# A ring of three score units in the attention stage, shared with the transposes

## The chip, the cores and the metric

The kernel runs on one core of a Trainium2 chip, as one launch. A core has a matrix engine (TensorE, PE in the views; its weight loads are the row PEld), a vector engine (VectorE, DVE), a scalar engine for activations (ScalarE, ACT), a general engine (GpSimd, POOL) and a queue that issues DMAs (SyncE, SP). Matrix products land in PSUM, which has eight banks; a bank holds 512 fp32 numbers on each of 128 partitions. The metric is the device time of one execution in microseconds; lower is better. Time before: 2411.94 us, the median of three runs (2408.89 to 2412.17).

## The reference

Four pre-norm residual blocks over x of 2 x 2048 tokens with 256 channels: a linear attention, a mixture of experts, a second attention, a second mixture of experts. The change lies in the second attention, a softmax attention with 16 heads of 16 channels:

```
v = _log_map(mu, x)
q = proj_h(v @ Wq.T); k = proj_h(v @ Wk.T); vv = heads(v @ Wv.T)
sc = (-q0 * k0 + q[..., 1:] . k[..., 1:]) / dh ** 0.5
at = softmax(sc, axis=-1)                  # 2048 x 2048 for each of 2 x 16 heads
out = einsum('bhqk,bhkc->bhqc', at, vv)
return _project(_exp_map(mu, out @ Wo.T))
```

So 32 matrices of 2048 x 2048 scores are made, exponentiated, and multiplied by the values.

## The kernel before, in words

The program is a row of stages with a barrier of all engines between them. `attention` (line 1534) is one stage; the stages before it and after it are not touched.

**Work and tiles.** The stage treats two heads at a time: 16 pairs, p = 0 to 15 (8 head pairs of each of 2 batches). A pair has 32 steps, and a step has two units n = 0 and 1. A unit is 128 keys against 512 queries of both heads, so 128 x 1024 scores in two PSUM banks. In all there are 16 x 32 x 2 = 1024 units. A unit goes through these operations:

- `scores` (L1699): two matmuls of 64 rows each (one for each head) write a unit of psS (L1706).
- ScalarE (L1800): one activation, the exponential, reads the unit from psS and writes it to pexp in SBUF, which has six places.
- `weigh` (L1710), once a step for both its units and two steps later: four products of the exponentials with the values (eight matmul records, since the data is fp32), accumulated in psO over the 16 tiles of keys (L1720). A column of ones among the values makes the denominators.

Step s of a pair has the key tile kt = s // 2 and the query half y = s % 2: both halves of the queries are accumulated side by side, each in its own bank of psO, psO[:, y, :].

**The shift of the softmax.** For each query tile of a later pair, one step makes one matmul of the queries with sums of keys (`means`, L1725, into the single bank psM), and VectorE takes its maximum (`reduce`, L1812). This runs six steps more than one pair ahead (AHEAD, `mean_at`). The sums of four keys each are made by `sum_keys` (L1807), one reduction over 2048 columns at step 10. When the 32 maxima of a pair are there, `make_shift` (L1826) computes the shift with four small operations at step 25 of VectorE's order, at step 28 `turn_shift` (L1748) transposes it on TensorE into psX, `put_shift` (L1838) copies it out, and SP writes it into the queries by two DMAs (L1682), before the pair begins.

**The output.** In step 1 of the next pair `take_out` (L1845) copies both banks of psO to SBUF, one after the other. In steps 3 and 5 `turn_out` (L1756) transposes a half with four transposes into psX, and `divide` (L1852) divides by the denominators and writes the result.

**Side work.** For the pairs 8 to 15, GpSimd (`high`, L1634) and VectorE (`low`, L1864) also split the weights of the last stage in two fp16 parts, one `low` in each of the steps 7, 9, 14, 16, 21 and 23 (SPLIT), with DMAs in and out by SP.

**Order.** The order is written out by hand, for each engine a loop over pairs and steps; every engine carries out its instructions in that order. TensorE's step (L1773 to L1786) is

```
scores(p, step, 0)
weigh(p, step - 2)          # or of the pair before, in steps 0 and 1
scores(p, step, 1)
means(q, n)                 # once a step
turn_out / turn_shift       # in a few steps
```

**Waits around the change.** psS has two units, and unit n of a step always lies in psS[:, n, :]. Before `scores` writes a unit, TensorE waits for the activation of the unit two before it (L1703, the count of `raised`, which starts at 2). `weigh` waits for both activations of its step (L1713) and, at the first key tile, for `take_out` of the bank that it will overwrite. `means` waits for the `reduce` before it (L1730). psX has one bank; the transposes of outputs and of the shift take turns in it, each waiting for `x_free` of the one before. PSUM is full: 4 banks psS, 2 psO, 1 psM, 1 psX.

Ahead of the loop, `first_means` and `first_reduce` make the shift of pair 0 and the first maxima of pair 1, with the banks of psS and psO as three buffers (`early`, L1607).

Of the kernel before, what the change touches and what calls it, by code (L numbers as in the profile page):

```python
# [23 lines left out]
P = 128  # L24
# [1509 lines left out]
def attention(nc, k):  # L1534
# [17 lines left out]
    AHEAD = 6  # L1552
    TURN = ST - 4
    SPLIT, SR = (7, 9, 14, 16, 21, 23), 3
    NSP = len(SPLIT)
# [3 lines left out]
    with Stage(nc, "at") as s:  # L1559
# [8 lines left out]
        inv = s.sb("inv", [P, 4, 4])  # L1568
        psS = s.ps("psS", [P, 2, UN])
        psO = s.ps("psO", [P, 2, BANK])  # L1570
        psM = s.ps("psM", [P, BANK])
        psX = s.ps("psX", [P, BANK])
        (scored, raised, weighed, v_ready, o_out, maxed, reduced, k_ready, shift_in, shifted, x_turned, x_free, chain,
# [22 lines left out]
        def uses():  # L1596
            order = [("shift", 0, 0)]
            for p in range(NPAIR):
                if p:
                    order += [("out", p - 1, 0), ("out", p - 1, 1)]  # L1600
                if p + 1 < NPAIR:
                    order += [("shift", p + 1, 0)]
            return {u: n for n, u in enumerate(order + [("out", NPAIR - 1, 0), ("out", NPAIR - 1, 1)])}

        x_use = uses()

        def early(at):  # L1607

            return (psS[:, 0, :], psS[:, 1, :], psO[:, :, :].rearrange("p a c -> p (a c)"))[at % 3].rearrange(
                "p (h c) -> p h c", h=2)  # L1610

# [9 lines left out]
        with nc.Block() as block:  # L1621
# [31 lines left out]
            def _(sp):  # L1653
# [24 lines left out]
                for p in range(NPAIR):  # L1678
                    sp.wait_ge(x_free, x_use["shift", p, 0] + 1)
                    for hh in range(2):  # L1680
                        row = hh * HR + ROW
                        sp.dma_start(keys(k.QT, p)[row:row + 1, :].rearrange("a (t c) -> a t c", c=P),  # L1682
                                     shiftT[hh * KT16:(hh + 1) * KT16, :]).then_inc(shift_in, 16)
                    if p == HPAIR:

                        sp.wait_ge(raised, 2 + (p - 1) * ST * 2)
# [10 lines left out]
            @block.tensor  # L1697
            def _(pe):
                def scores(p, step, n):  # L1699
                    kt, c = step // 2, (step % 2) * 2 + n  # L1700
                    u = (p * ST + step) * 2 + n

                    pe.wait_ge(raised, u + 1)  # L1703
                    for hh in range(2):
                        r = slice(hh * HR, (hh + 1) * HR)
                        mm = pe.matmul(psS[:, n, hh * BANK:(hh + 1) * BANK], keys(k.KT, p)[r, kt * P:(kt + 1) * P],  # L1706
                                       keys(k.QT, p)[r, c * BANK:(c + 1) * BANK], start=True, stop=True)
                    mm.then_inc(scored, 1)

                def weigh(p, step):  # L1710
                    kt, y = step // 2, step % 2

                    pe.wait_ge(raised, (p * ST + step) * 2 + 4)  # L1713
                    if kt == 0:
                        if p:
                            pe.wait_ge(o_out, 2 * (p - 1) + y + 1)
                        pe.wait_ge(v_ready, p + 1)
                    for g in range(4):
                        n, hh = g // 2, g % 2
                        mm = pe.matmul(psO[g * VW:(g + 1) * VW, y, :], vst[:, p % 2, hh, kt, :],  # L1720
                                       pexp[:, (p * ST + step) % 3 * 2 + n, hh * BANK:(hh + 1) * BANK],
                                       start=(kt == 0), stop=(kt == KT16 - 1))
                    mm.then_inc(weighed, 2)

                def means(p, n):  # L1725
                    if n == 0:
                        pe.wait_ge(k_ready, p + 1)
                    if p * ST + n:

                        pe.wait_ge(reduced, p * ST + n)  # L1730
                    hh, t = n % 2, n // 2
                    r = slice(hh * HR, (hh + 1) * HR)
                    pe.matmul(psM[:, :], keys(k.QT, p)[r, t * P:(t + 1) * P], ksumT[r, p % 2, :],  # L1733
                              start=True, stop=True).then_inc(maxed, 1)

                def first_means(p, t):
                    at = p * KT16 + t
                    if t == 0:
                        pe.wait_ge(k_ready, p + 1)
                    if at >= 3:  # L1740
# [7 lines left out]
                def turn_shift(p):  # L1748
                    pe.wait_ge(shifted, p + 1)
                    use = x_use["shift", p, 0]  # L1750
                    if use:
                        pe.wait_ge(x_free, use)
                    pe.transpose(psX[:, :].bitcast(F16)[0:ST, 0:P], shift[:, :, :].rearrange("p h t -> p (h t)"),
                                 k.identh[:, :]).then_inc(x_turned, 1)

                def turn_out(p, y):  # L1756
                    pe.wait_ge(o_out, 2 * p + y + 1)
                    pe.wait_ge(x_free, x_use["out", p, y])
                    for c in range(4):
                        mm = pe.transpose(psX[:, c * P:(c + 1) * P], oT[:, y, c * P:(c + 1) * P], k.ident[:, :])  # L1760
                    mm.then_inc(x_turned, 1)
# [9 lines left out]
                for p in range(NPAIR):  # L1771
                    pe.wait_ge(shift_in, 32 * (p + 1))
                    for step in range(ST):  # L1773
# [7 lines left out]
                        if q < NPAIR:  # L1781
                            means(q, n)
                        if step in (3, 5) and p:
                            turn_out(p - 1, step // 4)
# [4 lines left out]
                for y in range(2):  # L1789
                    turn_out(NPAIR - 1, y)  # L1790

            @block.scalar
            def _(act):
                act.sem_inc(raised, 2)

                for u in range(NPAIR * ST * 2):
                    act.wait_ge(scored, u + 1)

                    act.wait_ge(weighed, u + 1)
                    act.activation(pexp[:, u % 6, :], psS[:, u % 2, :], ACT.Exp,  # L1800
                                   scale=D ** -0.5 / (QS * QS)).then_inc(raised, 1)

            @block.vector
            def _(dve):
                dve.sem_inc(weighed, 6)

                def sum_keys(p):  # L1807
                    with nc.allow_low_precision(reason="the shift need not be exact"):
                        dve.tensor_reduce(ksumT[:, p % 2, :], keys(k.KT, p).rearrange("p (g m) -> p g m", m=GM),
                                          AX.X, ALU.add).then_inc(k_ready, 1)  # L1810

# [26 lines left out]
                def put_shift(p):  # L1838
                    dve.wait_ge(x_turned, x_use["shift", p, 0] + 1)
                    if p:  # L1840

                        dve.wait_ge(shift_in, 32 * p)
                    dve.tensor_copy(shiftT[:, :], psX[:, :].bitcast(F16)[0:ST, 0:P]).then_inc(x_free, 1)

                def take_out(p, y):  # L1845

                    dve.wait_ge(weighed, 6 + (p * ST + ST - 2 + y + 1) * 2)
                    if p:
                        dve.wait_ge(x_turned, x_use["out", p - 1, y] + 1)
                    dve.tensor_copy(oT[:, y, :], psO[:, y, :]).then_inc(o_out, 1)  # L1850

                def divide(p, y):  # L1852
                    dve.wait_ge(x_turned, x_use["out", p, y] + 1)
                    o = psX[:, :].rearrange("p (c g d) -> p c g d", c=4, g=4)
                    dve.reciprocal(inv[:, :, :], o[:, :, :, D]).then_inc(divided, 1)
# [12 lines left out]

                sum_keys(0)
                for t in range(KT16):  # L1870
                    if t == 2:
                        sum_keys(1)
                    first_reduce(0, t)
# [4 lines left out]
                for p in range(NPAIR):  # L1878
                    for step in range(ST):
                        if step == 1 and p:  # L1880
                            take_out(p - 1, 0)
                            take_out(p - 1, 1)
                        q, n = mean_at(p, step)
                        if q < NPAIR:
                            reduce(q, n)
                            if n == ST - 1:
                                make_shift(q)
                        if step == 10 and p + 2 < NPAIR:
                            sum_keys(p + 2)
                        if step in (3, 5) and p:  # L1890
# [5 lines left out]
                for y in range(2):  # L1896
                    take_out(NPAIR - 1, y)
                for y in range(2):
                    divide(NPAIR - 1, y)

# [452 lines left out]
```

## Time and profile before

| what | value |
|---|---|
| median of three runs | 2411.94 us |
| the profiled execution, its own time | 2414.36 us |
| its span, first to last instruction | 2412.6 us |
| mean granted TensorE clock | 0.938 |
| PE busy in the span | 2079.7 us (86%) |
| ACT busy in the span | 1534.8 us (64%) |
| DVE busy in the span | 1389.4 us (58%) |

The shares are means over stages with different limits, so they don't say what bounds the attention stage; for that one looks at the stretch of this stage by itself. All times are of one profiled execution, counted from the start of its span. A TensorE instruction appears twice: as PEld for its weight load, and as PE for the product. The ends of the products are modelled, so the starts are the better measure of how fast TensorE goes. An activation's record also covers its own latency, and it overlaps the next one's.

### The profile page before, as it was taken

The numbers are of one execution on the slowest core, as the hardware profiler recorded it, in microseconds if no ns is written. First come the engines' busy times: TensorE is split into PE (matmuls) and PEld (weight loads), VectorE is DVE, ScalarE is ACT, GpSimd is POOL, SyncE is SP. The second block draws the span as 40 slices with busy tenths as digits, with TensorE's granted clock in tenths as the row PEclk, the third lists the DMA queues.
The fourth block names the chain that finished last, engine by engine and source line by source line (L and its number), as shares of the span: only waits on it lengthen the run. The fifth ranks groups of instructions, "written<-read, shape, count | busy, mean of one in ns | idle before, by whom it ended". The sixth has DMA issues, their size and how long they took to land. (4 is left out here: it accounts for less than half of the span.)

```text
span 2412.6 us, 43912 instructions
## 1 busy us (share of the span) xinstructions
PE 2079.7 (86%) x13329; PEld 971.6 (40%) x13330; DVE 1389.4 (58%) x2986; ACT 1534.8 (64%) x2495; POOL 440.3 (18%) x678
## 2 busy tenths in 40 slices
PE   5997799950996999999999999999853699999992
PEld 4785455530661222222222222222242476766761
DVE  5567444347786444444445555553156687777774
ACT  2215333223774999999999999999862344444441
POOL 0030366642000000000000000000000134343430
PEclk9998899975996999999999999999976799999996
DMA  5001344443100000000002222222255265555656
GB/s 194 1 1 70 105 148 146 142 144 140 38 24 1 1 1 1 1 1 1 1 19 71 71 71 71 71 71 71 83 180 164 98 178 175 173 176 170 175 168 231
DMA packets 139075, 220.11 MB, mean 91 GB/s; under 512 B 14080, under 2 KB 108464, under 8 KB 138944
## 3 DMA queue, kind: packets, MB, share of 16 engines
q1 hardware_dynamic: 124160, 176.96, 23.6%
q0 software_dynamic: 13632, 37.24, 4.7%
q10 hardware_dynamic: 1152, 4.19, 0.4%
q8 instruction: 78, 1.28, 0.2%
q14 instruction: 53, 0.43, 0.1%
HBM read 161.82 MB, written 52.20 MB: 89 GB/s over the span
## 5 line engine op out<-in xcount | busy, mean ns | idle before, releaser
L1800 ACT ACTIVATE at_pexp<-at_psS 128x1024 f32<-128x1024 f32 x1024 | 964.2, 1023 | 42.9 <-PE at_psS L1706 39.8
L1814 DVE TENSOR_REDUCE at_mx<-at_psM 128x1 f32<-128x512 f32 x474 | 327.5, 691 | 464.3 <-PE at_psM L1733 464.3
L1720 PE MATMUL at_psO<-at_pexp,at_vst 128*32 128x512 f32 x4096 | 546.4, 605 | 0.1
L1706 PE MATMUL at_psS<-l1c_QT,l1c_KT 64*128 64x512 f16 x2048 | 403.6, 387 | 14.4 <-issue 5.6
L1706 PEld LDWEIGHTS at_psS<-l1c_QT,l1c_KT 64*128 64x128 f16 x2048 | 99.4, 92 | 632.4 <-ACT at_pexp L1800 598.9
L2136 PE MATMUL ex_psH<-wide_wgu,ex_xT 128*128 x1278 | 259.9, 357 | 0.2 <-issue 0.2
L2207 DVE SCALAR_TENSOR_TENSOR ex_bias<-ex_psH,top_w_scale,ex_bias 128x456 f32<-128x456 f32 x213 | 147.4, 692 | 76.7 <-PE ex_psH L2136 63.8
L988 POOL DMA_INDIRECT expert_rows<-ex_y,ex_odx x142 | 140.3, 988 | 259.5 <-issue 181.3
L2180 ACT ACTIVATE ex_sg<-ex_bias 128x228 f32<-128x228 f32 x213 | 83.7, 393 | 152.1 <-DVE ex_bias L2207 152.1
L1733 PE MATMUL at_psM<-at_ksumT,l1c_QT 64*128 64x512 bf16 x474 | 179.1, 378 | 0.6
L2136 PEld LDWEIGHTS ex_psH<-wide_wgu,ex_xT 128*128 128x128 f16 x1278 | 124.5, 97 | 111.8 <-issue 3.6
L982 POOL DMA_INDIRECT ex_xg<-normed,ex_idx x142 | 144.7, 1019 | 112.1 <-POOL ex_odx L973 99.3
L2159 PE MATMUL ex_psY<-wide_w2h,ex_hT 114*128 x1278 | 151.3, 272 | 1.1 <-DVE ex_y L2234 0.7
L1061 PE MATMUL ex_psH<-l_w,ex_xT 128*128 x284 | 141.3, 621 | 4.0 <-issue 2.7
L1626 POOL COPY at_vst<-wide_x 128x512 f32<-128x512 f32 x16 | 9.7, 609 | 675.9 <-PE at_psO L1720 675.9
L1720 PEld LDWEIGHTS at_psO<-at_pexp,at_vst 128*32 128x32 f32 x4096 | 80.6, 108 | 125.3 <-issue 123.6
L2159 PEld LDWEIGHTS ex_psY<-wide_w2h,ex_hT 114*128 114x128 f16 x1278 | 124.6, 98 | 15.7 <-issue 1.6
L1130 DVE TENSOR_SCALAR ex_y<-ex_psY,top_wgt 128x256 f32<-128x256 f32 x71 | 34.3, 484 | 139.5 <-PE ex_psY L1079 102.8
L1099 ACT ACTIVATE ex_hT<-ex_psG 128x256 f32<-128x256 f32 x71 | 27.3, 384 | 128.3 <-PE ex_psG L1070 128.3
L2192 ACT ACTIVATE ex_y<-ex_y,top_wgt 128x256 f32<-128x256 f32 x71 | 36.1, 508 | 93.5 <-DVE ex_y L2234 93.5
L2218 DVE TENSOR_TENSOR ex_h<-ex_bias,ex_sg 128x228 f32<-128x228 f32 x213 | 83.1, 390 | 11.1 <-ACT ex_sg L2180 11.0
L1639 POOL TENSOR_SCALAR l1c_KT<-l1c_KT,top_w_scale 128x684 f16<-128x684 f32 (+1 forms) x48 | 40.9, 859 | 245.4 <-DMA l1c_KT<-in_L_ffn_W 232.5
(362 smaller groups left out, 2782.6 us busy)
## 6 DMA issues: line engine op xcount, KB each, us to landing
ex_bias<-in_L_ffn_bg SPq DMA_DIRECT2D x71, 342.0 KB
ex_bias<-in_L_ffn_b SPq DMA_DIRECT2D x71, 342.0 KB
ex_piece<-in_L_ffn_W SPq DMA_DIRECT2D x48, 228.0 KB, 2.6
l1c_KT<-in_L_ffn_W SPq DMA_DIRECT2D x32, 342.0 KB, 3.4
halves<-l1c_KT SPq DMA_DIRECT2D x32, 342.0 KB, 3.3
wide_wgu<-halves SPq DMA_DIRECT2D x8, 1368.0 KB
ex_b<-in_L_ffn_b SPq DMA_DIRECT2D x71, 128.0 KB
normed<-rt_area SPq DMA_DIRECT2D x16, 512.0 KB, 2.6
```

The source lines that it names most:

```text
L982: pool.indirect_dma_start(xg[:, g, :], None, k.xn_d, bass.IndirectOffsetOnAxis(idx[:, g, :], 0)).then_inc(got[g], 16)
L988: pool.indirect_dma_start(k.y_d, bass.IndirectOffsetOnAxis(odx[:, j, :], 0), y[:, j, :], None).then_inc(put[j], 16)
L1061: mm = pe.matmul(psH[:, j, :], xT[:, j, kk, :], k.w13[:, ds(e, 1), kk, :].rearrange("p a c -> p (a c)"), start=(kk == 0), stop=(kk == KC - 1))
L1706: mm = pe.matmul(psS[:, n, hh * BANK:(hh + 1) * BANK], keys(k.KT, p)[r, kt * P:(kt + 1) * P], keys(k.QT, p)[r, c * BANK:(c + 1) * BANK], s ...
L1720: mm = pe.matmul(psO[g * VW:(g + 1) * VW, y, :], vst[:, p % 2, hh, kt, :], pexp[:, (p * ST + step) % 3 * 2 + n, hh * BANK:(hh + 1) * BANK] ...
L1733: pe.matmul(psM[:, :], keys(k.QT, p)[r, t * P:(t + 1) * P], ksumT[r, p % 2, :], start=True, stop=True).then_inc(maxed, 1)
L1800: act.activation(pexp[:, u % 6, :], psS[:, u % 2, :], ACT.Exp, scale=D ** -0.5 / (QS * QS)).then_inc(raised, 1)
L1814: dve.tensor_reduce(mx[:, n:n + 1], psM[:, :], AX.X, ALU.max).then_inc(reduced, 1)
L2136: mm = pe.matmul(psH[:, n, 0:G2].rearrange("p (n c) -> p n c", n=2), xT[:, j, x, kk, :], k.wgu[:, ds(e, 1), kk, :, w, n * HW:(n + 1) * HW] ...
L2159: mm = pe.matmul(psY[:, 0:C], hT[:, j, x, g, :], k.w2h[:, ds(e, 1), w, g, :].rearrange("p a c -> p (a c)"), start=(at == 0), stop=(at == l ...
L2180: act.activation(sg[:, n, :], bias[:, st.slot(1, BR), n, 0, :], ACT.Silu).then_inc(gated, 1)
L2207: dve.scalar_tensor_tensor(hb, psH[:, n, 0:G2].rearrange("p (n c) -> p n c", n=2), k.w_scale[:, 1:2], hb, ALU.mult, ALU.add).then_inc(adde ...
```

## The change

- psS has three units instead of two (RING = 3), used as a ring. The transposes of outputs and of shifts have no bank of their own any more: each takes the next unit of that ring. `uses` lists all uses of the ring in TensorE's order, and `unit_free` waits before each use for whatever used the same unit three uses earlier: the activation if it was scores, `x_free` if it was a transpose.
- A pair's steps go over all 16 key tiles for query half 0 and then for half 1: kt = step % 16, y = step // 16. So psO is one bank, accumulated for one half at a time.
- Half 0 is copied out in step 17 of its own pair, and transposed and divided in step 19; half 1 is copied in step 1 of the next pair, and transposed and divided in step 3. The first `weigh` of a half waits for the copy of the half before it. At the end of the last pair only one half is left.
- `sum_keys` makes a quarter of its columns in each of the steps 5, 6, 8 and 10 (SUMS) instead of all at step 10.
- psM and `means` stay as they are, one matmul a step. PSUM is full again: 6 banks psS, 1 psO, 1 psM. The first activation's waits are counted from zero instead of two.

```
-    psS = s.ps("psS", [P, 2, UN]);  psO = s.ps("psO", [P, 2, BANK]);  psX = s.ps("psX", [P, BANK])
+    psS = s.ps("psS", [P, RING, UN]);  psO = s.ps("psO", [P, BANK])

+    def uses():
+        order = []
+        for p in range(NPAIR):
+            for step in range(ST):
+                order += [("score", p, step * 2), ("score", p, step * 2 + 1)]
+                if step == OUT[1] and p:                # OUT = (19, 3)
+                    order.append(("out", p - 1, 1))
+                if step == OUT[0]:
+                    order.append(("out", p, 0))
+                if step == TURN and p + 1 < NPAIR:      # TURN = 28
+                    order.append(("shift", p + 1, 0))
+        return order + [("out", NPAIR - 1, 1)]

+    def unit_free(use):
+        v = place[use]
+        if v >= RING:
+            kind, p, n = order[v - RING]
+            if kind == "score":
+                pe.wait_ge(raised, p * ST * 2 + n + 1)
+            else:
+                pe.wait_ge(x_free, x_use[kind, p, n] + 1)

     def scores(p, step, n):
-        kt, c = step // 2, (step % 2) * 2 + n
-        pe.wait_ge(raised, u + 1)
+        kt, c = step % KT16, step // KT16 * 2 + n
+        unit_free(use)

     def weigh(p, step):
-        kt, y = step // 2, step % 2
+        kt, y = step % KT16, step // KT16
         if kt == 0:
-            if p:
-                pe.wait_ge(o_out, 2 * (p - 1) + y + 1)
+            if 2 * p + y:
+                pe.wait_ge(o_out, 2 * p + y)

     # VectorE's loop
     if step == 1 and p:
-        take_out(p - 1, 0)
         take_out(p - 1, 1)
+    if step == KT16 + 1:
+        take_out(p, 0)
...
-    if step == 10 and p + 2 < NPAIR:
-        sum_keys(p + 2)
+    if step in SUMS and p + 2 < NPAIR:
+        sum_keys(p + 2, SUMS.index(step), SUMS.index(step) + 1)
-    if step in (3, 5) and p:
-        divide(p - 1, step // 4)
+    if step == OUT[1] and p:
+        divide(p - 1, 1)
+    if step == OUT[0]:
+        divide(p, 0)
```

## Rows read from the trace of the kernel before

**Rows 1.** Busy time by stretch: length, PE, PEld, DVE, ACT, POOL, clock, DMA, GB/s.
```profile
760.76:1738.10 977.34, 967.81 (x6743) 202.35 (x6740) 450.69 (x732) 964.20 (x1024) 49.25 (x62) 1.00 0.12 36
1745.00:2412.00 667.00, 529.09 (x3642) 376.32 (x3640) 480.95 (x1039) 282.68 (x740) 178.80 (x285) 0.90 0.56 173
```
**Rows 2.** Groups of instructions, 755 to 1745: busy, mean ns, idle before.
```profile
L1800 ACT ACTIVATE at_pexp<-at_psS 128x1024 f32<-128x1024 f32 x1024 | 964.2, 1023 | 42.9 <-PE at_psS L1706 39.8
L1720 PE MATMUL at_psO<-at_pexp,at_vst 128*32 128x512 f32 x4096 | 546.4, 605 | 0.1
L1814 DVE TENSOR_REDUCE at_mx<-at_psM 128x1 f32<-128x512 f32 x474 | 327.5, 691 | 464.3 <-PE at_psM L1733 464.3
```
**Rows 3.** Waits, 755 to 1745: us in total, times, longest.
```profile
PEld at_psS L1706 <- ACT at_pexp L1800: 598.9, 904, 1.7
ACT at_pexp L1800 <- PE at_psS L1706: 39.8, 32, 29.8
PEld at_psM L1733 <- DVE at_mx L1814: 4.8, 14, 0.3
```
**Rows 4.** The activations of L1800 from 956 to 1017: durations, first and last start.
```profile
L1800 ACT ACTIVATE at_pexp<-at_psS x65: 1017/1024/1043, 955.5 to 1016.6; 128x1024 f32<-128x1024 f32 x65
```
**Rows 5.** Timeline of ACT: start, length, count; an overlapping run is one row.
```profile
1005.72 4.77 ACT L1800 ACTIVATE at_pexp<-at_psS 128x1024 f32<-128x1024 f32 x5
...
1008.54 1.03 ACT L1800 ACTIVATE at_pexp<-at_psS 128x1024 f32<-128x1024 f32 x1
...
1018.93 1.02 ACT L1800 ACTIVATE at_pexp<-at_psS 128x1024 f32<-128x1024 f32 x1 [0.29 <-PE at_psS L1706]
...
1019.85 1.02 ACT L1800 ACTIVATE at_pexp<-at_psS 128x1024 f32<-128x1024 f32 x1
...
1020.75 1.03 ACT L1800 ACTIVATE at_pexp<-at_psS 128x1024 f32<-128x1024 f32 x1
```
**Rows 6.** Timeline, step 1 of a pair, with its copies of psO.
```profile
1006.78 0.10 PEld L1706 LDWEIGHTS at_psS<-l1c_QT,l1c_KT 64*128 64x128 f16 x2 [0.39 <-ACT at_pexp L1800]
...
1007.11 0.16 PEld L1720 LDWEIGHTS at_psO<-at_pexp,at_vst 128*32 128x32 f32 x8 [0.23 <-issue]
...
1007.53 1.40 DVE L1850 COPY at_oT<-at_psO 128x512 f32<-128x512 f32 x2
1008.10 0.10 PEld L1706 LDWEIGHTS at_psS<-l1c_QT,l1c_KT 64*128 64x128 f16 x2 [0.84 <-ACT at_pexp L1800]
```
**Rows 7.** Timeline, the transposes of step 5 and the step after.
```profile
1016.28 0.38 PE L1733 MATMUL at_psM<-at_ksumT,l1c_QT 64*128 64x512 bf16 x1
1016.59 0.42 PEld L1760 LDWEIGHTS at_psX<-top_ident,at_oT 128*128 128x128 f32 x4 [0.42 <-issue]
...
1017.17 0.10 PEld L1706 LDWEIGHTS at_psS<-l1c_QT,l1c_KT 64*128 64x128 f16 x2 [0.17 <-issue]
...
1017.59 0.49 DVE L1859 TENSOR_TENSOR wide_x<-at_psX,at_inv 128x128 f32<-128x128 f32 x2
1018.49 0.10 PEld L1706 LDWEIGHTS at_psS<-l1c_QT,l1c_KT 64*128 64x128 f16 x2 [0.84 <-ACT at_pexp L1800]
...
1020.24 0.10 PEld L1706 LDWEIGHTS at_psS<-l1c_QT,l1c_KT 64*128 64x128 f16 x2 [0.84 <-ACT at_pexp L1800]
```
**Rows 8.** Timeline, step 28: means, the shift's transpose, the next score.
```profile
998.84 0.38 PE L1733 MATMUL at_psM<-at_ksumT,l1c_QT 64*128 64x512 bf16 x1
...
999.30 0.10 PEld L1706 LDWEIGHTS at_psS<-l1c_QT,l1c_KT 64*128 64x128 f16 x2
```
**Rows 9.** VectorE's sums of keys and splits; landing of L1682's DMAs.
```profile
L1809 DVE TENSOR_REDUCE at_ksumT<-l1c_KT 128x512 bf16<-128x2048 f16 x14 | 31.9, 2276 | 0.0
...
L1866 DVE SCALAR_TENSOR_TENSOR l1c_KT<-l1c_KT,top_w_scale x48: 919/922/1019, 1265.9 to 1703.4; 128x684 f16<-128x684 f32 x32, 114x768 f16<-114x768 f32 x16
...
DMA to landing us min/median/max: 1.6/1.7/2.9
```
**Rows 10.** Timeline, the end of the stage: last copy, last transposes.
```profile
1739.27 0.69 DVE L1850 COPY at_oT<-at_psO 128x512 f32<-128x512 f32 x1 [0.49 <-PE at_psO L1720]
...
1740.76 0.42 PEld L1760 LDWEIGHTS at_psX<-top_ident,at_oT 128*128 128x128 f32 x4 [1.21 <-DVE at_oT L1850]
```

More of the change, by code:

```diff
@@ L1553, in attention @@
     TURN = ST - 4
+    OUT = (KT16 + 3, 3)
+    RING = 3
+    SUMS = (5, 6, 8, 10)
     SPLIT, SR = (7, 9, 14, 16, 21, 23), 3
@@ L1596, in uses @@
         def uses():
-            order = [("shift", 0, 0)]
+            order = []
             for p in range(NPAIR):
-                if p:
[L1600 to L1605, printed above, removed]
+                for step in range(ST):
[7 more added lines that the diff above has]
+            return order + [("out", NPAIR - 1, 1)]
+        order = uses()
+        unit = {use: v % RING for v, use in enumerate(order)}
+        x_use = {use: n for n, use in enumerate([("shift", 0, 0)] + [v for v in order if v[0] != "score"])}
+        unit["shift", 0, 0] = (KT16 + AHEAD // 2) % RING
+        place = {use: v for v, use in enumerate(order)}
         def early(at):
-            return (psS[:, 0, :], psS[:, 1, :], psO[:, :, :].rearrange("p a c -> p (a c)"))[at % 3].rearrange(
-                "p (h c) -> p h c", h=2)
+            return psS[:, at % RING, :].rearrange("p (h c) -> p h c", h=2)
         def keys(stack, p):
@@ L1698, in _ @@
             def _(pe):
+                def unit_free(use):
[6 more added lines that the diff above has]
+                            pe.wait_ge(x_free, x_use[kind, p, n] + 1)
                 def scores(p, step, n):
-                    kt, c = step // 2, (step % 2) * 2 + n
-                    u = (p * ST + step) * 2 + n
-                    pe.wait_ge(raised, u + 1)
+                    kt, c = step % KT16, step // KT16 * 2 + n
+                    use = "score", p, step * 2 + n
+                    unit_free(use)
                     for hh in range(2):
                         r = slice(hh * HR, (hh + 1) * HR)
-                        mm = pe.matmul(psS[:, n, hh * BANK:(hh + 1) * BANK], keys(k.KT, p)[r, kt * P:(kt + 1) * P],
+                        mm = pe.matmul(psS[:, unit[use], hh * BANK:(hh + 1) * BANK], keys(k.KT, p)[r, kt * P:(kt + 1) * P],
                                        keys(k.QT, p)[r, c * BANK:(c + 1) * BANK], start=True, stop=True)
@@ L1749, in turn_shift @@
                     pe.wait_ge(shifted, p + 1)
[L1750 to L1753, printed above, removed]
+                    if p:
+                        unit_free(("shift", p, 0))
+                    else:
+                        pe.wait_ge(reduced, 2 * (KT16 + AHEAD // 2 - RING) + 2)
+                    pe.transpose(psS[:, unit["shift", p, 0], :].bitcast(F16)[0:ST, 0:P], shift[:, :, :].rearrange("p h t -> p (h t)"),
                                  k.identh[:, :]).then_inc(x_turned, 1)
@@ L1757, in turn_out @@
                     pe.wait_ge(o_out, 2 * p + y + 1)
-                    pe.wait_ge(x_free, x_use["out", p, y])
+                    unit_free(("out", p, y))
                     for c in range(4):
-                        mm = pe.transpose(psX[:, c * P:(c + 1) * P], oT[:, y, c * P:(c + 1) * P], k.ident[:, :])
+                        mm = pe.transpose(psS[:, unit["out", p, y], c * P:(c + 1) * P], oT[:, y, c * P:(c + 1) * P], k.ident[:, :])
                     mm.then_inc(x_turned, 1)
@@ L1788, in _ @@
                 weigh(NPAIR - 1, ST - 1)
-                for y in range(2):
-                    turn_out(NPAIR - 1, y)
+                turn_out(NPAIR - 1, 1)
             @block.scalar
             def _(act):
-                act.sem_inc(raised, 2)
                 for u in range(NPAIR * ST * 2):
@@ L1799, in _ @@
                     act.wait_ge(weighed, u + 1)
-                    act.activation(pexp[:, u % 6, :], psS[:, u % 2, :], ACT.Exp,
+                    act.activation(pexp[:, u % 6, :], psS[:, unit["score", u // (ST * 2), u % (ST * 2)], :], ACT.Exp,
                                    scale=D ** -0.5 / (QS * QS)).then_inc(raised, 1)
@@ L1805, in _, with sum_keys @@
                 dve.sem_inc(weighed, 6)
-                def sum_keys(p):
+                def sum_keys(p, first, last):
+                    g = TS // GM // 4
                     with nc.allow_low_precision(reason="the shift need not be exact"):
-                        dve.tensor_reduce(ksumT[:, p % 2, :], keys(k.KT, p).rearrange("p (g m) -> p g m", m=GM),
-                                          AX.X, ALU.add).then_inc(k_ready, 1)
+                        dve.tensor_reduce(ksumT[:, p % 2, first * g:last * g],
+                                          keys(k.KT, p)[:, first * g * GM:last * g * GM].rearrange("p (g m) -> p g m", m=GM),
+                                          AX.X, ALU.add).then_inc(k_ready, last - first)
                 def reduce(p, n):
@@ L1887, in _ @@
                                 make_shift(q)
[L1888 to L1891 removed]
+                        if step in SUMS and p + 2 < NPAIR:
+                            sum_keys(p + 2, SUMS.index(step), SUMS.index(step) + 1)
+                        if step == OUT[1] and p:
+                            divide(p - 1, 1)
+                        if step == OUT[0]:
+                            divide(p, 0)
                         if step in SPLIT and p >= HPAIR:
@@ L1895, in _ @@
                             put_shift(p + 1)
[L1896 to L1899, printed above, removed]
+                take_out(NPAIR - 1, 1)
+                divide(NPAIR - 1, 1)
 def attention_out(nc, k, meanwhile):
```

31 lines of the change are left out of this document (15 added, 16 removed).

## The prediction

> **What bounds the kernel now.** I read the busy times by stretch first, because the change touches one stage. That stage runs from 760.8 to 1738.1, and in its 977.3 us ScalarE is busy for 964.2 [rows 1]. TensorE looks as busy (967.8), but its ends are modelled, so this alone doesn't say who leads. The waits do: TensorE's score loads waited 904 times for an activation to give a unit back, 598.9 us in all, while the activations waited visibly for scores 32 times [rows 3]; 29.8 of those 39.8 us are the wait before the first one, so about 10 us lie inside. The clock was granted at 1.00 (2.4 GHz) throughout [rows 1].
>
> The visible waits understate the loss. An activation's record (1.02 us) overlaps the next one, so one that starts 0.07 late leaves no idle time. So I looked at starts. From 955.5 to 1016.6 there are 65 activations, so one pair (64 units) takes 61.1 us, 0.955 a unit [rows 4]. But the start after a waiting activation came 0.92 later (1018.93 to 1019.85), and the start after one that had not waited 0.90 later (1019.85 to 1020.75) [rows 5]. At these pitches a pair would take 57.9 to 58.9. So 2.2 to 3.2 us of each pair, 35 to 51 in the stage, are late scores.
>
> **Where they come from.** With two units, the first score of a step waits for the end of the activation two units earlier. Then comes the chain: 0.05 from that end (1005.72 plus the 1.02 of its length) to the score at 1006.78; 0.33 to `weigh` at 1007.11; 0.99 to the second score at 1008.10 [rows 6]; 0.44 to its activation at 1008.54 [rows 5]. From the start of one activation to the start of the third after it, this loop takes 2.82. Three free pitches are 2.74 (at 0.9125, the middle). So the loop is a little too long, and every second unit is pinned by it. On top come the transposes: TensorE's path from `means` at 1016.28 to the next score at 1017.17 takes 0.89 [rows 7], where it is about 0.19 without them (a loaded step is 1.75 from second score to second score, 1018.49 to 1020.24 [rows 7]; less 0.99 + 0.33 of rows 6 and 0.23 from score to `means`). A set of transposes costs TensorE 0.70, and an idle ScalarE 0.29 visibly [rows 5].
>
> **Part 1, the third unit.** The first score of a step now waits for the activation three units earlier, and `weigh` of step s - 2 needs that same activation. The loop of 2.82 now spans four pitches, 3.65. So TensorE may be 0.83 late before ScalarE notices. What is next behind it is TensorE's own work: 32 steps x 1.75 = 56.0, two sets of transposes at 0.70 = 1.4, and the shift's transpose: 998.84 to 999.30 is 0.46 [rows 8], 0.27 over 0.19. Together 57.7 a pair, against ScalarE's 58.4. ScalarE stays the bound, but by 0.7 of 58, and a step recovers only 1.825 - 1.75 = 0.075 of lateness.
>
> **Part 2, transposes in the ring.** A transpose borrows a unit, so the next step's first score has again to wait for the activation two before it: lateness 0.91 at once, 0.08 over the margin. That is a stall of 0.09 at step 29, and 0.09 at step 20, whatever TensorE's own 0.27 or 0.70 (they lie inside that wait). At step 3 it is worse: step 29 left a lateness of 0.83, six steps take off 0.45, the half's boundary adds 0.07 (part 3), the transposes 0.70: 1.15, over the margin by 0.32. Stalls of a pair: 0.09 + 0.09 + 0.32 = 0.50. The borrowed unit is free once `divide` ends: transposes at 1016.59, last multiply over at 1018.08 [rows 7], 1.5 later. The score that needs it is two steps on, at 0.58 + 1.75 = 2.3 after the transposes' start. So 0.8 of cover; without it a late `divide` costs its excess over 0.8 + 0.83, 31 times. The shift's unit is held by one small copy and has more cover. Its DMAs land in at most 2.9 [rows 9], with more than three steps (5.5) to go; TensorE's being earlier by less than one unit doesn't use this up.
>
> **Part 3, one bank of output.** The first `weigh` of a half must wait for the copy of the half before it, whose last `weigh` is one step back. The second copy in rows 6 ends at 1008.93 (1007.53 + 1.40), 1.82 after the `weigh` at 1007.11 that it waited for; with some 0.06 to the next load the two `weigh` stand 1.88 apart. A free step is 1.825 and a loaded one 1.75, so this adds 0.06 to 0.13 of lateness, inside the margin except at step 3, counted above. Behind the waiting `weigh` on TensorE are the second score and `means`; ScalarE waits for that score. In pairs 8 to 15, step 16 on VectorE also has a `low` of 0.92 to 1.02 [rows 9] after a reduction of 0.69 [rows 2]. I reckon that it can push the copy by 0.4; the lateness at step 18 is then still inside 0.83, but the transposes of step 19 bring it to about 1.17, 0.25 more stall, in 8 pairs at most 2 us. I take 0 to 2, and 0 in the sum, because by step 17 the lateness of step 4 is worked off. Number and length of copies, transposes and divides are unchanged, and TensorE's products too (a half accumulates 16 tiles in either order).
>
> **Part 4, key sums in quarters.** One sum took 2.28 on VectorE, 14 times [rows 9], and `means` waited 0.34 behind it each time, 4.8 in all [rows 3]. A quarter is an estimated 0.57 plus up to 0.1; with the reduction 1.4, under a step. In the new ring even the old stall would mostly have been covered, so the gain is 0 to 2 and I count it inside the pair's 2.2.
>
> **Part 5, the end.** The last half was copied by 1739.96, but its transposes began at 1740.76, behind the other half's divide [rows 10]. Only one half is left: 0.7 gained (0 to 0.8). Ahead of the loop the same number of reductions runs in the same order: 0.
>
> **The sum.** Per pair 58.4 + 0.5 = 58.9 against 61.1: 2.2, times 16 = 35.2, plus 0.7: 35.9. From the profiled execution's 2414.4 that leaves 2378.5; it was 2.4 above the median of the runs, so 2376 stands against 2411.9. Bounds: with a pitch of 0.904 and the stalls that its smaller margin gives (0.65 a pair) it is 58.5, 42 saved, 2370; with 0.921, 59.3, 29.5 saved, 2382. TensorE's step is the other unknown: 1.75 is read from loaded steps of two, and each 0.01 more costs 0.3 a pair once TensorE leads; at 1.79 it is 57.7 + 1.3, plus 0.3 for waits on the ring that it can't use (an estimate, half of the stalls above): 59.3 a pair, 2382. The stage after is 667 us at a clock of 0.90 [rows 1]; where its low stretches fall can move it by a few us either way. I take the middle of the pitches, since activations that wait and ones that don't will both occur.
>
> **A rule against the change.** The starts just read give 0.90 to 0.92. The Trainium skill (ScalarE: Activation LUTs, What ACT_TABLE_LOAD costs) gives an activation with immediate scale 186 ns + 0.833 ns an element, with 93 ns of overlap back to back. For 1024 elements that is an estimated pitch of 0.946, so the stage would have only 8 us to give, and the time would be about 2403. The trace doesn't agree: its pitches are 0.03 to 0.04 shorter, and its mean with all stalls is 0.955.
>
> **Rivals.**
> *A: TensorE becomes the bound.* A step costs 1.81 to 1.85 where TensorE never rests, because products that were spread out now queue. For: its total of 57.7 is within 0.7 of ScalarE's. Against: the loaded steps of rows 7 were just such. Price: 32 x 0.06 to 0.10 on the 57.7 and the 0.3, so 59.9 to 61.2 a pair, saving 20 to nothing: 2392 to 2412. Chance 0.12.
> *B: the exponential itself is slower when fed densely.* For: the run of five has (4.77 - 1.03) / 4 = 0.935 [rows 5]; 1023 x 0.935 = 956.5, 20 saved, 2392 (the page's rule above would be this rival's far end). Against: that run contains pinned units, and the shorter pitches stand alone beside it. Chance 0.06.
> *C: slower.* The ring is blocked by VectorE: the scores two steps after a transpose wait for `divide`, which stands behind reductions, splits and copies in VectorE's order. To lose the whole gain, each of the 31 borrowings must cost 1.2 more, so `divide` must end some 2.8 later than it did. Above that it is slower: at 3.0 late, 31 x (3.0 - 1.63) = 42 more than forecast, 2418. For: nothing else waits in so long a circle. Against: VectorE is busy 450.7 of 977 [rows 1] and no `low` stands in steps 3 or 19. Chance 0.04.
>
> **How the numbers follow.** Forecast 0.78, A 0.12, B 0.06, C 0.04. The forecast's own range is 2368 to 2386; of A and B I take in the nearer parts: 2366 to 2394. Less than 0.2% (about 5 us) can't be told from no change. Faster by more than that: all of the forecast and B, most of A, 0.93; same 0.04 (the end of A, a part of C); slower 0.03.
>
> **What would show it.** Right: the stage's 977 falls to about 941; activations start 0.90 to 0.92 apart in most steps; visible idle of ScalarE stays near steps 4, 20 and 29; loads of scores wait much less for activations in the steps after a transpose; no `means` waits for a reduction. Wrong: loads with almost no wait at all and steps over 1.8 (A); unwaited starts over 0.93 (B); TensorE waiting for line 1859's multiply (C).

## The result: 1.4% faster, and the profile after

The changed kernel takes 2378.07 us (median of four runs, 2374.1 to 2380.22) against 2411.18 for the kernel before in the same comparison. The ratio is 0.9862, with a 95% interval of 0.9845 to 0.9879. 2376 had been forecast, within 2366 to 2394. The profiled execution took 2380.22, with a span of 2378.5.

First the stretch of the activations in the kernel after (columns as in [rows 1]), then its groups and waits, which answer to [rows 2, 3]:

```profile
763.28:1708.70 945.42, 927.90 (x6751) 204.78 (x6747) 454.96 (x777) 942.80 (x1024) 49.20 (x62) 1.00 0.12 37
```
```profile
L1820 ACT ACTIVATE at_pexp<-at_psS x1024: 1018/1138/1458, 763.3 to 1707.3; 128x1024 f32<-128x1024 f32 x171
```
```profile
PEld at_psS L1724 <- ACT at_pexp L1820: 497.7, 705, 1.7
...
ACT at_pexp L1820 <- PE at_psS L1724: 32.4, 16, 29.9
...
PEld at_psM L1752 <- DVE at_mx L1836: 0.4, 1, 0.4
```

From the first to the last start of an activation it was 976.3 us (760.8 to 1737.1 before), and it is 944.0: 32.3 less. The rest of the span's 34.1: the stretch ahead of the first activation got 2.5 longer (760.8 to 763.3), the one after the last start 4.3 shorter (675.5 to 671.2). Of that, about 0.5 is the one half that is left at the end of the stage: the last multiply ends 4.7 after the last activation's start, where it was 5.2. The remainder lies in stages that weren't changed.

The activations' visible waits fell from 32 to 16, of which one is the 29.9 before the first; the other 15, one for each pair from the second on, make 2.5 together. The mean's wait for its reduction went from 4.8 to 0.4, and the score loads' waits for activations from 598.9 to 497.7. The copy of a half, and the two `weigh` that it stands between:

```profile
970.66 0.16 PEld L1739 LDWEIGHTS at_psO<-at_pexp,at_vst 128*32 128x32 f32 x8 [0.23 <-issue]
...
971.80 0.69 DVE L1872 COPY at_oT<-at_psO 128x512 f32<-128x512 f32 x1 [0.64 <-PE at_psO L1739]
...
972.56 0.19 PEld L1739 LDWEIGHTS at_psO<-at_pexp,at_vst 128*32 128x32 f32 x8 [0.29 <-issue]
```

They are 1.90 apart, where 1.88 was worked out.

**What a start doesn't tell.** One pair now runs from 940.5 to 999.6, 59.1 us for 64 units, against 61.1 [rows 4]. Single activations of that pair, each row with its start and length:

```profile
L1820 ACT ACTIVATE at_pexp<-at_psS x65: 1018/1138/1405, 940.5 to 999.6; 128x1024 f32<-128x1024 f32 x65
```
```profile
945.95 1.15 ACT L1820 ACTIVATE at_pexp<-at_psS 128x1024 f32<-128x1024 f32 x1
...
946.85 1.17 ACT L1820 ACTIVATE at_pexp<-at_psS 128x1024 f32<-128x1024 f32 x1
...
947.78 1.15 ACT L1820 ACTIVATE at_pexp<-at_psS 128x1024 f32<-128x1024 f32 x1
...
949.10 1.02 ACT L1820 ACTIVATE at_pexp<-at_psS 128x1024 f32<-128x1024 f32 x1 [0.17 <-PE at_psS L1724]
...
976.22 1.41 ACT L1820 ACTIVATE at_pexp<-at_psS 128x1024 f32<-128x1024 f32 x1
...
977.20 1.34 ACT L1820 ACTIVATE at_pexp<-at_psS 128x1024 f32<-128x1024 f32 x1
...
978.51 1.02 ACT L1820 ACTIVATE at_pexp<-at_psS 128x1024 f32<-128x1024 f32 x1
```

After a stall a record is 1.02 long; then each next one starts 0.903 later but is 0.013 longer, up to 1.41. The ends, which is when a unit is given back, are 0.917 apart. From 976.22 to 977.20 to 978.51 the starts jump by 0.98 and 1.31, but the ends (977.63, 978.54, 979.53) only by 0.91 and 0.99: most of the jump is the drift falling back. Read by ends, a pair has 64 x 0.917 = 58.7 plus three stalls: 0.27 at step 4 (948.93 to 950.12 is 1.19; the expectations below round it to 0.28), 0.08 at step 20, 0.08 at step 29.

**What a pair lost before.** Read the same way, a pair of the kernel before has 58.7 plus 2.4. Activations of its fourth pair and of the start of the fifth:

```profile
961.56 1.02 ACT L1800 ACTIVATE at_pexp<-at_psS 128x1024 f32<-128x1024 f32 x1
...
964.32 1.02 ACT L1800 ACTIVATE at_pexp<-at_psS 128x1024 f32<-128x1024 f32 x1
...
965.30 1.02 ACT L1800 ACTIVATE at_pexp<-at_psS 128x1024 f32<-128x1024 f32 x1
...
1013.42 1.02 ACT L1800 ACTIVATE at_pexp<-at_psS 128x1024 f32<-128x1024 f32 x1
...
1014.74 1.02 ACT L1800 ACTIVATE at_pexp<-at_psS 128x1024 f32<-128x1024 f32 x1 [0.29 <-PE at_psS L1706]
```

From 961.56 to 965.30 four units take 3.74, where four paces are 3.67; the 0.08 falls on one of the four, 13 times a pair, about 1.0 us in all. The two sets of transposes cost 1.1 (one late activation is 1013.42 to 1014.74: 1.32, 0.40 too much), the shift's transpose 0.18 and the wait behind the whole key sum 0.13. So the loop of two units alone is less than half of what was lost; the rest is detours that it had no margin for.

### The profile page after: what moved, and what is told of

Its sections match the earlier page's. It is cut to its first block and busy times, and to the rows that moved or that the text cites. A ratio compares the mean times of both kernels' runs of the same rounds, so it can differ in the third digit from the quotient of the medians.

```text
span 2378.5 us, 43954 instructions
## 1 busy us (share of the span) xinstructions
PE 2036.8 (86%) x13329; PEld 972.3 (41%) x13330; DVE 1392.7 (59%) x3028; ACT 1513.1 (64%) x2495; POOL 439.6 (18%) x678
## 5 line engine op out<-in xcount | busy, mean ns | idle before, releaser
L1820 ACT ACTIVATE at_pexp<-at_psS 128x1024 f32<-128x1024 f32 x1024 | 942.8, 1161 | 32.4 <-PE at_psS L1724 32.4
L1724 PE MATMUL at_psS<-l1c_QT,l1c_KT 64*128 64x512 f16 x2048 | 412.6, 384 | 17.9 <-ACT at_pexp L1820 9.8
L1724 PEld LDWEIGHTS at_psS<-l1c_QT,l1c_KT 64*128 64x128 f16 x2048 | 105.3, 93 | 537.7 <-ACT at_pexp L1820 498.5
L2247 DVE SCALAR_TENSOR_TENSOR ex_hT<-ex_psG,top_w_scale,ex_hT 114x384 f16<-114x384 f32 x142 | 81.1, 613 | 6.2 <-ACT ex_hT L2209 1.0
```

Source lines behind the costliest of these rows:

```text
L1724: mm = pe.matmul(psS[:, unit[use], hh * BANK:(hh + 1) * BANK], keys(k.KT, p)[r, kt * P:(kt + 1) * P], keys(k.QT, p)[r, c * BANK:(c + 1) * ...
L1820: act.activation(pexp[:, u % 6, :], psS[:, unit["score", u // (ST * 2), u % (ST * 2)], :], ACT.Exp, scale=D ** -0.5 / (QS * QS)).then_inc( ...
```

## The experiments

The measure is the time from the first to the last start of an activation, since the other stages scatter by a few us; one pair is given as well, read by the same view as [rows 4]. The kernel before has 976.3 and 61.1, the one after 944.0 and 59.1. From the first to the last end, as some expectations count it, it is the same for the kernels before, with two units' waits and with halves only, 0.6 more with the transposes in the means' bank and 0.3 more for the others. The last column is the median where a ratio is given below, and one run otherwise.

| kernel | activations, us | a pair (the fourth) | time, us |
|---|---|---|---|
| two units' waits, one more wait | 997.3 | 62.4 | 2431.1 |
| two units' waits, clean | 978.7 | 61.1 | 2413.3 |
| halves only | 980.3 | 61.3 | 2411.9 |
| whole sums | 944.7 | 59.1 | 2378.0 |
| one more matmul a mean | 954.2 | 59.7 | 2386.2 |
| slow divide | 980.9 | 61.4 | 2414.1 |
| transposes in step 12 | 945.5 | 59.1 | 2371.7 |
| transposes in step 9 | 942.4 | 58.9 | 2369.3 |
| transposes in the means' bank | 954.1 | 59.8 | 2389.2 |
| spread | 941.1 | 58.9 | 2376.1 |
| spread, shift in the means' bank | 940.3 | 58.8 | 2371.5 |
| the changed kernel again | 944.1 | 59.1 | 2375.5 |

**Is it the third unit?** In the changed kernel, a score also waits as if there were two units.

```
 def scores(p, step, n):
     unit_free(use)
+    if (p * ST + step) * 2 + n >= 2:
+        pe.wait_ge(raised, (p * ST + step) * 2 + n - 1)
```

> The changed kernel with its three units, but every score also waits for the activation two units before it, as with two units. Theory (the third unit makes the gain by making TensorE's loop span four pitches instead of three): every second unit is pinned again, a step goes from 1.83 back to about 1.87 us, and the transposes cost 0.4 each again; a pair takes 61.0 to 61.4 us, the stage's activations 976 to 979 us from first to last start, the time 2408 to 2412 us. Rival (the order by halves, one output bank and the smaller sums make the gain): a pair stays at 59.1 and the time at about 2378.

Measured: ratio to the kernel before 1.0079 (1.0062 to 1.0096), 997.3 us. The whole gain is gone, but 18 to 21 us more than the theory allows went with it. So the wait was made single (only the new lines are shown; they take the place of `unit_free(use)`):

```
+    if v >= RING and order[v - RING][0] != "score":
+        unit_free(use)
+    if u >= 2:
+        pe.wait_ge(raised, u - 1)
```

> The changed kernel with two units' waits, as before, but a score has one wait for an activation and not two in a row (the second wait only where the unit was lent to a transpose). Theory (in the first form of this experiment, 997 us, the second wait instruction lay on the loop and cost some 0.09 a time, on top of the two-unit loop): the loop is 2.82 again, pinned units come 0.995 and not 1.085 after the one before them, and the activations take 976 to 981 us. Rival (something else in the new order costs the 20 us): 990 or more.

Measured 978.7, a pair 61.1: two units' waits take the whole gain back, and with them the late activations at the loop's 0.08 and behind the transposes; and the 18.6 us between the two forms are the second wait. Load of a score and of the `weigh` after it, first with two waits, then with one:

```profile
964.01 0.13 PEld L1726 LDWEIGHTS at_psS<-l1c_QT,l1c_KT 64*128 64x128 f16 x2 [0.54 <-ACT at_pexp L1822]
964.36 0.14 PEld L1741 LDWEIGHTS at_psO<-at_pexp,at_vst 128*32 128x32 f32 x6 [0.23 <-issue]
```
```profile
961.84 0.10 PEld L1728 LDWEIGHTS at_psS<-l1c_QT,l1c_KT 64*128 64x128 f16 x2 [0.47 <-ACT at_pexp L1824]
962.16 0.14 PEld L1743 LDWEIGHTS at_psO<-at_pexp,at_vst 128*32 128x32 f32 x6 [0.23 <-issue]
```

Score to `weigh` is 0.35 instead of 0.32. The activation waited for was the second of this run of two with two waits (the run ends 1.94 after its start):

```profile
961.96 1.94 ACT L1822 ACTIVATE at_pexp<-at_psS 128x1024 f32<-128x1024 f32 x2
```

It ended at 963.90, so the load came 0.11 later; with one wait the same gap was 0.05 (961.79 to 961.84). Together 0.09 each time the loop goes round.

**Does the order by halves do a part?** The kernel before with only the order changed.

```
-kt, c = step // 2, (step % 2) * 2 + n
+kt, c = step % KT16, step // KT16 * 2 + n
-kt, y = step // 2, step % 2
+kt, y = step % KT16, step // KT16
```

with the copies, transposes and divides in the steps of the changed kernel.

> The kernel before with only the order changed: key tiles for half 0, then for half 1, with copies in steps 17 and 1 and transposes in steps 19 and 3; still two score units, two output banks and a bank for the transposes. Theory (the loop of 2.82 us with two units is the bound whatever the order): a pair stays within 0.3 us of 61.1, and the time within 5 us of 2411. Rival (the order makes part of the gain): a pair of 60 or less, 2394 or less.

Measured: 980.3, a pair 61.3, ratio 1.0013 (1.0004 to 1.0022). Alone, the order gains nothing; it costs 4 us of the stage. It is what makes room: it frees the bank of psO.

**Key sums in one piece.**

```
-if step in SUMS and p + 2 < NPAIR:
-    sum_keys(p + 2, SUMS.index(step), SUMS.index(step) + 1)
+if step == 10 and p + 2 < NPAIR:
+    sum_keys(p + 2, 0, 4)
```

> The changed kernel with the key sums of a pair made whole at step 10 again (one reduction of 2.28 us). Theory (a stall of means behind the sum is inside TensorE's margin of 0.83 us): 0 to 0.2 us a pair, activations 944 to 947 us from first to last start. Rival (the quarters were needed): the 0.34 to 0.45 us come back at step 12 or 13 in each of 14 pairs, 949 to 951.

Measured 944.7, 0.7 more. The quarters are worth less than 1 us once the third unit is there. Most of the 0.7 lies in six of the later pairs: in the eleventh, the ends before and after the stall of step 20 are 1.08 apart, where they are 1.00 in the changed kernel.

**How much room has TensorE?** Before each mean one more matmul of 128 columns.

```
+pe.matmul(psM[:, 0:128], keys(k.QT, p)[r, t * P:(t + 1) * P], ksumT[r, p % 2, 0:128],
+          start=True, stop=True)
```

> The changed kernel with one more matmul of 128 columns before each mean (its result is overwritten). Theory (TensorE's step of 1.75 and 57.7 us a pair leave 1.0 to ScalarE's 58.7): with some 0.06 more a step TensorE comes to 59.6 a pair and leads, so a pair is 59.8 to 60.2, and the activations take 955 to 958 us from first to last start instead of 944. Rival (the 1.75 holds waiting that extra work could fill): 944 to 947.

Measured 954.2, a pair 59.7: the first theory, a little below its range. Loaded steps in this kernel:

```profile
946.20 0.10 PEld L1724 LDWEIGHTS at_psS<-l1c_QT,l1c_KT 64*128 64x128 f16 x2 [0.84 <-issue]
...
948.01 0.11 PEld L1724 LDWEIGHTS at_psS<-l1c_QT,l1c_KT 64*128 64x128 f16 x3 [0.84 <-ACT at_pexp L1822]
...
949.81 0.10 PEld L1724 LDWEIGHTS at_psS<-l1c_QT,l1c_KT 64*128 64x128 f16 x2 [0.84 <-ACT at_pexp L1822]
```

and in the changed kernel:

```profile
950.41 0.11 PEld L1724 LDWEIGHTS at_psS<-l1c_QT,l1c_KT 64*128 64x128 f16 x3 [0.84 <-ACT at_pexp L1820]
...
952.16 0.10 PEld L1724 LDWEIGHTS at_psS<-l1c_QT,l1c_KT 64*128 64x128 f16 x2 [0.84 <-ACT at_pexp L1820]
```

A step is 1.80 to 1.81 where it was 1.75, so about 1.8 us a pair was added, and the pair grew by 0.6 (by 0.8 in the pairs 8 to 15, 59.9). So 1.0 to 1.2 of the 1.8 found room; 58.7 - 57.7 = 1.0 by the sum of TensorE's work. The growth stands at the old places: the stalls of steps 4 and 20 are 0.6 and 0.3 now, and everywhere else the ends stay 0.917 apart. In the changed kernel TensorE is close behind ScalarE.

**Rival C's price.** One reduction more inside `divide`, ahead of the multiplies that give the unit back.

```
+dve.tensor_reduce(junk[:, :], batch((p + HPAIR) % NPAIR)[:, 0:8, :]
+                  .rearrange("p t (g m) -> p (t g) m", m=8), AX.X, ALU.add)
```

> The changed kernel with one more reduction of 2048 fp32 (an estimated 2.2 to 2.3 us) inside each divide, before the unit is given back. By the prediction's cover (0.8 to the score that needs the unit, 0.83 of margin) each of 31 divides would cost 0.6 to 0.7, 20 us in all, 964. By the lateness that the trace after shows (the margin is already used up when the unit was borrowed) only the 0.8 covers, so each costs 1.2 to 1.5, 37 to 46 us: 981 to 990 from first to last start. If VectorE has room that neither counts, 944 to 950.

Measured 980.9; the reduction takes 2.29 in the trace and a pair grew by 2.36: 1.31 in step 5 and 1.04 in step 21 of the fourth pair, two steps behind the transposes, 1.18 on average. So only about 1.1 of the 2.29 was covered, not the 1.63 of the prediction. That is the second of the three expected cases, at its lower edge.

**Where the last 0.27 comes from.** The second half's transposes and divide moved from step 3 to 9, and to 12: `OUT = (KT16 + 3, 9)` and `OUT = (KT16 + 3, 12)`.

> The changed kernel with the second half's transposes and divide in step 9 instead of 3. Theory (the stall of 0.28 at step 4 is lateness left over from the shift's transpose of step 28, which TensorE works off by 0.08 a step): with 12 steps between, and 10 to step 19, only 0.08 is left at each of steps 10, 20 and 29, so a pair is 58.9 instead of 59.09 and the activations take 941 to 942 us from first to last start (up to 944 if the splits of pairs 8 to 15 in step 9 delay VectorE). Rival (the stall belongs to a transpose wherever it stands): 944.3 as before, with 0.28 at step 10.

> The same with step 12 instead of 3, so that only 7 steps lie between it and step 19. Theory (lateness left over): the 0.28 moves to step 20, where it was 0.08, and step 13 has 0.08; a pair stays at 59.1 us and the activations at 944 to 947. Rival (the stall comes from the copy of a half just before its transposes in steps 1 to 3): with the transposes far from the boundary it goes, 58.9 a pair, 941 to 942, like step 9.

In the kernel with step 9, the activations before and after the stalls of steps 10 and 20:

```profile
953.14 1.32 ACT L1820 ACTIVATE at_pexp<-at_psS 128x1024 f32<-128x1024 f32 x1
...
954.43 1.02 ACT L1820 ACTIVATE at_pexp<-at_psS 128x1024 f32<-128x1024 f32 x1
...
971.62 1.24 ACT L1820 ACTIVATE at_pexp<-at_psS 128x1024 f32<-128x1024 f32 x1
...
972.84 1.02 ACT L1820 ACTIVATE at_pexp<-at_psS 128x1024 f32<-128x1024 f32 x1
```

and with step 12, of steps 13 and 20:

```profile
959.27 1.34 ACT L1820 ACTIVATE at_pexp<-at_psS 128x1024 f32<-128x1024 f32 x1
...
960.59 1.02 ACT L1820 ACTIVATE at_pexp<-at_psS 128x1024 f32<-128x1024 f32 x1
...
972.37 1.15 ACT L1820 ACTIVATE at_pexp<-at_psS 128x1024 f32<-128x1024 f32 x1
...
973.69 1.02 ACT L1820 ACTIVATE at_pexp<-at_psS 128x1024 f32<-128x1024 f32 x1 [0.17 <-PE at_psS L1724]
```

The ends with step 9 are 0.99 and 1.00 apart, so 0.08 each; with step 12 they are 1.00 apart at step 13 and 1.19 at step 20. The 0.27 has moved to the next event that comes within seven steps, so it is lateness left over from the one before. The copy at the half's boundary and the transposes don't make it alone: in the changed kernel step 19 has both ahead of it, and its stall is 0.08. In pairs 8 to 15 the kernel with step 9 still took 59.0 instead of 58.9, the one with step 12 59.3 instead of 59.1.

**All transposes in the bank of the means.** Issued between the first score and `weigh` of steps 3, 19 and 28, the ring for scores alone, and VectorE's divide ahead of its reduction of that step (abridged):

```
 scores(p, step, 0)
+if turned:
+    mean_free(p, step)          # waits for the reduction of the step before
+    turn_out(...) or turn_shift(...)      # into psM
 weigh(...)
 scores(p, step, 1)
+if turned:
+    pe.wait_ge(x_free, x_use[turned] + 1)
 means(q, n)
```

> The changed kernel with all transposes in the bank of the means (psM) instead of a score unit, issued between the first score and weigh of the step, so that weigh hides VectorE's divide before the means need the bank; the ring of three is for scores alone. Theory (the stalls left, 0.28 + 0.08 + 0.08 a pair, come from the borrowed unit and the lateness that it leaves, and TensorE has 1 us to spare a pair): none of them stays, a pair is 58.7 us (64 ends of activations 0.917 apart), the activations take 938 us from first to last end, and the time is about 6 us below 2378. Rival (TensorE's own work of transposes makes them): a stall of 0.1 to 0.3 stays after each output transpose, 941 to 944, and no clear gain.

Measured: ratio 0.9919 (0.9905 to 0.9932), 954.1: 10 us worse than the changed kernel. Neither theory had it. The trace shows what was left out:

```profile
973.88 0.69 DVE L1841 TENSOR_REDUCE at_mx<-at_psM 128x1 f32<-128x512 f32 x1 [1.14 <-PE at_psM L1754]
974.62 0.42 PEld L1777 LDWEIGHTS at_psM<-top_ident,at_oT 128*128 128x128 f32 x4 [0.87 <-DVE at_mx L1841]
974.63 0.66 PE L1777 MATMUL at_psM<-top_ident,at_oT 128*128 128x128 f32 x4 [0.57 <-DVE at_mx L1841]
975.21 0.16 PEld L1741 LDWEIGHTS at_psO<-at_pexp,at_vst 128*32 128x32 f32 x8 [0.17 <-issue]
```
```profile
976.64 1.02 ACT L1825 ACTIVATE at_pexp<-at_psS 128x1024 f32<-128x1024 f32 x1 [0.29 <-PE at_psS L1726]
```

The bank holds the last step's mean until its reduction ends at 974.57, and TensorE, with `weigh` and the second score behind it, stood still for 0.57. That and the transposes' 0.59 lie in the chain to the second score; the stall is 0.39 by ends at step 19 (starts 974.94 and 976.64 with lengths 1.42 and 1.02), and 0.70 at step 3, where by the account above lateness was left.

**A better version.** Transposes in step 9, and the splits moved away from the half's boundary and from step 9: `SPLIT = (7, 11, 13, 15, 21, 23)`. In a second kernel the shift's transpose is also put in the bank of the means, but behind `weigh` of step 28, where the reduction has ended.

> The changed kernel with the second half's transposes in step 9 instead of 3, and the six splits of a pair in the steps 7, 11, 13, 15, 21 and 23 instead of 7, 9, 14, 16, 21 and 23, so that none stands in VectorE's order just before the copy of step 17. Theory (the 0.14 that the pairs 8 to 15 still lose at step 20 with the transposes in step 9 is that split of step 16 delaying the copy): all pairs take 58.89 us, the activations 941.3 us from first to last end, the time 2375, 3 below the changed kernel. Rival (it is VectorE's load in these pairs as a whole): pairs 8 to 15 stay at 59.03, 942.6.

> The same, and the shift's transpose uses the bank of the means in step 28, between weigh and the second score, so that it borrows no score unit. Theory (a borrowed unit costs 0.08 because the next first score must wait for the activation two before it, 2.83 us against three pitches of 2.75): the 0.08 at step 29 goes, 58.81 a pair, 940.1 us. Rival (TensorE's own 0.27 and its wait for the copy cost as much): 941.3 or more.

> The changed kernel once more, on the same chip and in the same rounds as the two others, so that they can be compared: 2378 us, 944.3 us of activations from first to last end.

One of the later pairs (the eleventh), first with the transposes in step 9 alone, then spread:

```profile
L1820 ACT ACTIVATE at_pexp<-at_psS x65: 1017/1130/1318, 1347.6 to 1406.6; 128x1024 f32<-128x1024 f32 x65
```
```profile
L1820 ACT ACTIVATE at_pexp<-at_psS x65: 1018/1138/1338, 1345.4 to 1404.3; 128x1024 f32<-128x1024 f32 x65
```

The pair goes from 59.0 to 58.9, and the activations take 941.1; which of the moved splits did it can't be told, since three moved at once. With the shift's transpose out of the ring they take 940.3: a pair is 58.8, and the 0.08 at step 29 is gone, so it came from the borrowed unit. The stages are 3.0 and 3.8 us shorter than in the changed kernel measured beside them. The ratios to the kernel before are 0.9864 (0.9847 to 0.9880), 0.9835 (0.9815 to 0.9855), and 0.9857 (0.9841 to 0.9873) for the changed kernel: their intervals overlap, so that the whole program is faster than the changed kernel is not shown by them; that the stage is shorter is. The four runs of the last kernel (2365.2 to 2372.5) do all lie below the four of the changed kernel beside them (2375.0 to 2380.4), by 3.9 in the median, which fits the stage's 3.8.

## Why the prediction was right, step by step

- **What bounds it.** Right that it was the two units: with their waits the changed kernel is back at 61.1 a pair. But the loop of 2.82 didn't pin every second unit. It bound at one unit in four, 0.08 each time, about 1.0 us a pair of the 2.4 lost; the transposes, which the prediction only put "on top", cost 1.1, and the rest was the shift and the key sum. The forecast of the gain didn't depend on this split, since it was taken from the whole 61.1.
- **Part 1, the third unit.** Right in mechanism, and the 57.7 us of TensorE's work fit what one more matmul found of room. The pace of ScalarE was mis-sized: 0.9125 was taken as the middle of 0.904 and 0.921, both read from starts [rows 5]. By ends it is 0.917. 64 x 0.0042 is 0.27 a pair, 4.3 us in all.
- **Part 2, the stalls.** 0.09, 0.09 and 0.32 were worked out, 0.08, 0.08 and 0.27 were measured, at the forecast steps; 1.1 us in all the other way. 976.3 - 35.2 = 941.1 had been forecast; 941.1 + 4.3 - 1.1 is 944.3, and by ends it was 944.3. The rule behind them, that a borrowed unit leaves a lateness of a little over 0.8 that goes down by 0.08 a step, held in both moved versions.
- **Part 3.** Right: 1.90 for 1.88. The up to 2 us from the split of step 16 did not appear in the changed kernel (its later pairs also take 59.1). The later pairs lost more only where TensorE was already later: 0.14 to 0.2 a pair with the transposes in step 9 or 12 and with one more matmul, 0.1 with whole sums and the slow divide. With three splits moved it went, but that it is the one of step 16 is not shown.
- **Part 4.** Right, at the low end: under 1 us.
- **Part 5.** 0.7 expected, about 0.5 seen. The other stages, put at 0, gave 1.3 (4.3 - 0.5 - 2.5). That is luck, inside their scatter, and it brought the time nearer to the forecast.
- **The rule against the change.** The 0.946 that the prediction estimated for an activation's pace from the Trainium skill (ScalarE: Activation LUTs, What ACT_TABLE_LOAD costs) did not hold. It was 0.917 over long unstalled runs. The pace isn't as low as the starts of [rows 5] suggested either.
- **Rivals.** A, 59.9 or more a pair, is out at 59.1, but near: under 0.06 us a step more gave 59.7. B is out in its size (0.935), though the pace was indeed longer than the starts showed. C didn't occur, and its cover was overestimated: 1.63 was the sum of the 0.8 and the margin, but the borrowed unit itself had already used the margin. With 1.1 of cover the point from which it is slower lies near the slow divide, which came out at 2414.
- **What would show it.** The stretch of the stage fell to 945, not to about 941, for the pace of ScalarE. A mean still waited for a reduction, once. One sign was wrong: visible idle of ScalarE was to stay near steps 4, 20 and 29. It stayed at step 4 only, since long records hide the 0.08 of the other two.

## What to carry to other kernels

A ring's depth is worth the loop that it lengthens: add up the chain from the start of the use that releases a unit to the start of the use that this can delay, and compare it with the paces of the bound engine between the two (here three with two units, four with three). What the chain is too long is lost each time that it binds, and with no margin so is every detour in it, here the transposes; one unit more gives both back, up to its margin. Whoever borrows a unit of the ring takes that margin away for a while, so events that borrow belong as far apart as the engine behind needs to catch up. A bank that looks free in the schedule has to be followed to the end of its last reader in the trace, in microseconds and not in steps: the bank of the means held TensorE up by 0.57.

## What the runs showed of the hardware

- Activations that never wait have records whose starts come 0.903 apart and grow by 0.013 each; the pace is that of their ends, 0.917. After a stall the length falls back to 1.02. So neither the gaps of starts nor the visible idle time measures a stall; the ends do.
- A wait instruction in front of a matmul that already waits isn't free on a critical loop: 0.06 before the score's load and 0.03 up to the next load, 18.6 us over the stage.
